# A state space layer on partition halves: two states stacked, channel halves side by side, sums by 64-column matmuls

## What is computed

```
xz = x @ W_in                                  # 256 -> 2 x 512
xc, z = split(xz)
xc = silu(causal_conv4(xc) + conv_b)
proj = xc @ W_xproj                            # 16 + 16 (B) + 16 (C)
dt = softplus(proj_dt @ W_dt + b_dt)           # 512 channels
A = -exp(A_log)                                # 512 x 16
h[t] = h[t-1] * exp(dt[t] * A) + dt[t] * xc[t] * B[t]      # 512 channels x 16 states
y[t] = sum over states (h[t] * C[t]) + D * xc[t]
out = (y * silu(z)) @ W_out
```

## Time and profile before

| | |
|---|---|
| Median of 3 runs | 3203.89 us (3202.26 to 3206.14) |
| Profiled execution, its own time | 3204.56 us |
| Its span | 3203.0 us |
| Busy over the span | PE 2843.9 (89%), PEld 1845.6, VectorE 2080.0 (65%), ACT 1471.0, POOL 1509.9 |
| Granted TensorE clock, mean | 0.957 |
| State space layer's items | from 40.07 to about 1017 us |

### The profile page before, as it was taken

The page is one execution under the profiler, slowest core; times in us unless marked ns, Lnnn a source line. Parts: engine busy times, 40 slices in busy tenths (PEclk is TensorE's granted clock), DMA queues, the critical chain, the costliest instruction groups (busy, mean ns, idle before and its releaser), DMA issues. The chain is left out here.

```text
span 3203.0 us, 41427 instructions
## 1 busy us (share of the span) xinstructions
PE 2843.9 (89%) x14210; PEld 1845.6 (58%) x14210; DVE 2080.0 (65%) x3833; ACT 1471.0 (46%) x2768; POOL 1509.9 (47%) x1192
## 2 busy tenths in 40 slices
PE   6898998998977877899999999978877999999998
PEld 2343343343333664555555555546666888888887
DVE  7899999999998654677777777758863222222221
ACT  5667667666763301366666656545541111111111
POOL 5788788888785553133333333256752111111111
PEclk8999999999999788899999999999888999999999
DMA  7135145145140162212322222110115665556662
GB/s 233 51 108 159 46 116 160 35 125 159 34 136 1 41 211 94 81 42 65 81 63 65 58 50 64 50 59 29 50 63 198 200 203 183 181 181 187 205 199 60
DMA packets 283856, 346.32 MB, mean 108 GB/s; under 512 B 85788, under 2 KB 238552, under 8 KB 283592
## 3 DMA queue, kind: packets, MB, share of 16 engines
q1 hardware_dynamic: 260399, 310.17, 31.3%
q0 software_dynamic: 16704, 27.21, 3.6%
q10 hardware_dynamic: 6544, 6.30, 0.7%
HBM read 234.69 MB, written 107.95 MB: 107 GB/s over the span
## 5 line engine op out<-in xcount | busy, mean ns | idle before, releaser
L542 POOL TENSOR_TENSOR mb_drive<-mb_dtx,mb_b_rep 128x1024 f32<-128x1024 f32 x255 | 597.0, 2355 | 179.9 <-DVE mb_pD L439 87.9
L853 PE MATMUL mb_pY<-mb_hc,ident 128*128 128x512 f32 x1024 | 502.9, 616 | 55.9 <-DVE mb_hc L456 55.5
L1981 DVE TENSOR_REDUCE at_nm_of<-at_pS 128x1 f32<-128x128 f32 (+1 forms) x756 | 401.6, 556 | 135.8 <-PE at_pS L1969 75.8
L3153 POOL DMA_INDIRECT out<-et_y,et_to x71 | 112.0, 1577 | 667.0 <-DVE et_y L3207 411.0
L3197 DVE TENSOR_TENSOR et_mT<-et_silu,et_pU 128x512 f32<-128x512 f32 (+1 forms) x160 | 100.3, 628 | 471.2 <-ACT et_silu L3168 471.1
L3168 ACT ACTIVATE et_silu<-et_pG 128x512 f32<-128x512 f32 (+1 forms) x160 | 87.8, 549 | 658.0 <-PE et_pU L3229 658.0
L853 PEld LDWEIGHTS mb_pY<-mb_hc,ident 128*128 128x128 f32 x1024 | 190.3, 195 | 326.9 <-issue 183.3
L1969 PE MATMUL at_pS<-at_kT,at_qT 128*128 128x128 f32 (+1 forms) x756 | 306.3, 407 | 65.3 <-DVE at_nm_of L1981 53.4
L598 ACT ACTIVATE mb_pD<-mb_dt,mb_a_neg 128x512 f32<-128x512 f32 x384 | 259.6, 688 | 157.3 <-DVE mb_hc L456 146.0
L439 DVE TENSOR_TENSOR_SCAN mb_pD<-mb_pD,mb_drive 128x1024 f32<-128x1024 f32 x128 | 292.7, 2287 | 42.9 <-ACT mb_pD L596 40.2
L445 DVE TENSOR_TENSOR_SCAN mb_pD<-mb_pD,mb_carried,mb_drive 128x512 f32<-128x512 f32 x256 | 314.0, 1271 | 6.8 <-ACT mb_pD L598 6.8
(11 more groups left out here) (491 smaller groups left out, 4984.7 us busy)
## 6 DMA issues: line engine op xcount, KB each, us to landing
t_wg<-in_t_wgT SPq DMA_DIRECT2D x40, 1024.0 KB, 6.3
t_wu<-in_t_wuT SPq DMA_DIRECT2D x40, 1024.0 KB, 8.8
t_wd<-in_t_wdT SPq DMA_DIRECT2D x40, 1024.0 KB, 11.3
mb_b_rep<-mb_rows SPq DMA_DIRECT2D x64, 512.0 KB, 5.6
mb_c_rep<-mb_rows SPq DMA_DIRECT2D x64, 512.0 KB, 4.8
t_h_sorted<-blank SPq DMA_DIRECT2D x6, 4160.0 KB, 20.2
t_h_sorted<-blank SPq DMA_DIRECT2D x18, 1170.0 KB, 6.2
t_h_sorted<-blank SPq DMA_DIRECT2D x12, 1040.0 KB, 5.8
```

Source lines behind the costliest of these rows:

```text
L542: nc.gpsimd.tensor_tensor(drive[G % RINGS][:, :, :], dtx[:, m, :].unsqueeze(1).to_broadcast([P, 2, CH]), b_rep[:, 2 * j:2 * j + 2, :], ALU ...
L853: last = nc.tensor.matmul(pY[:, :], K.ident[:, :], hc[G % RINGS][:, k, :], start=False, stop=(j == PAIRS - 1 and k == 1))
L1981: nc.vector.tensor_reduce(nm_of[t % 2][:, w0 // 512, a, qb:qb + 1], score_bank(t, k)[:, 0:w1 - w0], axis=AX.X, op=ALU.max, negate=True).th ...
```

## The change

An item's two states now lie on the two partition halves (state 2j on partitions 0 to 63, state 2j+1 on 64 to 127), and the tile's two channel halves lie side by side where the two states lay. Then:

- a row of B or C goes to 64 partitions only: `b_rep` and `c_rep` are half as large, and are filled by two transfers of 128 KB each where there was one of 512 KB; the second operand of drive and weighting is repeated over the channel halves;
- dt and dtx are needed as [2 copies on the partition halves, channel half, 512]. They are copied there from SBUF to SBUF, into `dt2` and `dtx2` with TWINS = 3 buffers, by `twins`: four transfers of 128 KB for dt and four for dtx, for each of the 32 tiles. SP issues tile 0's of the next chunk behind the transfers of j = 5, and those of tiles 1 to 3 behind `fill_rows`;
- decay and drive wait for these copies in place of dt and dtx;
- `state_sum` multiplies with `fold` (128 x 64, the sum of the identity's two halves), once for each channel half, into partitions 0 to 63 and 64 to 127 of `pY`; the skip product is split likewise;
- `step_sizes` of the next chunk's tile 0 moves from s = 31 to s = 29;
- A_log is laid out for this on the host.

```diff
+    HP = P // 2
+    TWINS = 3
@@
-        a_neg = sb("a_neg", [P, ME, NST])
+        a_neg = sb("a_neg", [P, ME, 2, PAIRS])
+        fold = sb("fold", [P, HP])
@@
-        b_rep, c_rep = sb("b_rep", [P, NST, CH]), sb("c_rep", [P, NST, CH])
+        dt2, dtx2 = sb("dt2", [P, TWINS, 2, CH]), sb("dtx2", [P, TWINS, 2, CH])
+        b_rep, c_rep = sb("b_rep", [P, PAIRS, CH]), sb("c_rep", [P, PAIRS, CH])
@@ SP
+            def twins(ch, m):
+                nth = ch * ME + m
+                q = nth % TWINS
+                for made, to, s_made, s_to, s_used, per in ((dt, dt2, s_dt, s_dt2, s_dec, 2), (dtx, dtx2, s_dtx, s_dtx2, s_drv, 1)):
+                    eng.wait_ge(s_made, nth + 1)
+                    if nth >= TWINS:
+                        eng.wait_ge(s_used, (nth - TWINS + 1) * PAIRS * per)
+                    for k in range(2):
+                        for h in range(2):
+                            eng.dma_start(to[h * HP:(h + 1) * HP, q, k, :], made[k * HP:(k + 1) * HP, m, :]).then_inc(s_to[q], 16)
@@
-                    eng.dma_start(b_rep[:, 2 * j:2 * j + 2, :], rows_dram[ch % 2][2 * j:2 * j + 2, :].partition_broadcast(P)).then_inc(s_b[j], 16)
+                    for h in range(2):
+                        eng.dma_start(b_rep[h * HP:(h + 1) * HP, j, :], rows_dram[ch % 2][2 * j + h, :].partition_broadcast(HP)).then_inc(s_b[j], 16)
                     if ch > 0:
                         eng.wait_ge(s_hc, last_user + 1)
-                    eng.dma_start(c_rep[:, 2 * j:2 * j + 2, :],
-                                  rows_dram[ch % 2][NST + 2 * j:NST + 2 * j + 2, :].partition_broadcast(P)).then_inc(s_c[j], 16)
+                    for h in range(2):
+                        eng.dma_start(c_rep[h * HP:(h + 1) * HP, j, :], rows_dram[ch % 2][NST + 2 * j + h, :].partition_broadcast(HP)).then_inc(s_c[j], 16)
+                    if j == 5:
+                        twins(ch, 0)
                 fill_rows(K, eng, K.h1_sorted, ch, NCH, s_fill)
+                for m in range(1, ME):
+                    twins(ch, m)
@@ drive (VectorE for item 0, POOL for the others)
+        def twin_made(eng, s_to, nth):
+            eng.wait_ge(s_to[nth % TWINS], 64 * (nth // TWINS + 1))
+
+        def drive_of(unit, ch, m, j, r):
+            return unit.tensor_tensor(drive[r][:, :, :], dtx2[:, (ch * ME + m) % TWINS, :, :],
+                                      b_rep[:, j, :].unsqueeze(1).to_broadcast([P, 2, CH]), ALU.mult)
@@ weigh
-                nc.vector.tensor_tensor(hc[r][:, :, :], pD[r][:, :, :], c_rep[:, 2 * j:2 * j + 2, :], ALU.mult).then_inc(s_hc, 1)
+                nc.vector.tensor_tensor(hc[r][:, :, :], pD[r][:, :, :], c_rep[:, j, :].unsqueeze(1).to_broadcast([P, 2, CH]), ALU.mult).then_inc(s_hc, 1)
@@ VectorE, start
+            nc.vector.tensor_tensor(fold[:, :], K.ident[:, 0:HP], K.ident[:, HP:P], ALU.add).then_inc(s_fold, 1)
@@ POOL, drives
                 if j == 0 or G == 1:
-                    eng.wait_ge(s_dtx, ch * ME + m + 1)
+                    twin_made(eng, s_dtx2, ch * ME + m)
@@ POOL, loop
-                    if s == 31 and ch + 1 < NCH:
+                    if s == 29 and ch + 1 < NCH:
                         step_sizes(eng, nc.gpsimd, ch + 1, 0)
@@ ACT, decay
-                scale = a_neg[:, m, 2 * j + k:2 * j + k + 1]
+                scale = a_neg[:, m, k, j:j + 1]
+                step = dt2[:, (ch * ME + m) % TWINS, k, :]
                 if k == 0:
                     if j == 0:
-                        eng.wait_ge(s_dt, ch * ME + m + 1)
+                        twin_made(eng, s_dt2, ch * ME + m)
@@ ACT, magnitude
                 if ch > 0:
-                    eng.wait_ge(s_drv, (ch - 1) * ITEMS + (m + 1) * PAIRS)
+                    twin_made(eng, s_dt2, (ch - 1) * ME + m)
+                    twin_made(eng, s_dtx2, (ch - 1) * ME + m)
@@ PE, state_sum
-                    nc.tensor.matmul(pY[:, :], skip[:, m, :], xc(ch, m), start=True, stop=False)
+                    for k in range(2):
+                        nc.tensor.matmul(pY[k * HP:(k + 1) * HP, :], skip[:, m, k * HP:(k + 1) * HP], xc(ch, m), start=True, stop=False,
+                                         skip_group_check=True)
                 eng.wait_ge(s_hc, G + 1)
                 for k in range(2):
-                    last = nc.tensor.matmul(pY[:, :], K.ident[:, :], hc[G % RINGS][:, k, :], start=False, stop=(j == PAIRS - 1 and k == 1))
+                    last = nc.tensor.matmul(pY[k * HP:(k + 1) * HP, :], fold[:, :], hc[G % RINGS][:, k, :], start=False, stop=(j == PAIRS - 1),
+                                            skip_group_check=True)
```

More of the change, by code:

```diff
@@ L288, in mamba @@
             sem(n) for n in ("dec", "drv", "scan", "keep", "hc", "y", "fin", "rows", "fill"))
+        s_dt2, s_dtx2 = [sem(f"dt2_{q}") for q in range(TWINS)], [sem(f"dtx2_{q}") for q in range(TWINS)]
+        s_fold = sem("fold")
         s_b = [sem(f"b{j}") for j in range(PAIRS)]
@@ L321, in _ @@
                 loads.append((dst[:, :], io[name].rearrange("(m p) -> p m", p=P)))
-            loads += [(a_neg[:, :, :], io["mb_A_log"].rearrange("(m p) n -> p m n", p=P)),
+            loads += [(a_neg[:, :, :, :].rearrange("p m k j -> p (m k j)"), io["mb_A_log"]),
                       (w_x[:, :, :], io["mb_w_x"].rearrange("(m p) n -> p m n", p=P)),
@@ L349, in _ @@
             for j in range(PAIRS):
-                eng.wait_ge(s_b[j], 16 * NCH)
-                eng.wait_ge(s_c[j], 16 * NCH)
-        ALL_IN = 16 * 7
+                eng.wait_ge(s_b[j], 32 * NCH)
+                eng.wait_ge(s_c[j], 32 * NCH)
+            for q in range(TWINS):
+                uses = len(range(q, NCH * ME, TWINS))
+                eng.wait_ge(s_dt2[q], 64 * uses)
+                eng.wait_ge(s_dtx2[q], 64 * uses)
+        ALL_IN = 16 * 7
+        def twin_made(eng, s_to, nth):
[3 more added lines that the diff above has]
+                                      b_rep[:, j, :].unsqueeze(1).to_broadcast([P, 2, CH]), ALU.mult)
         def normalise(eng, unit, ch):
@@ L426, in first_drive @@
             def first_drive():
[L427 to L430, removed]
+                twin_made(eng, s_dtx2, 0)
+                eng.wait_ge(s_b[0], 32)
+                drive_of(nc.vector, 0, 0, 0, 0).then_inc(s_drv, 1)
             def scans(G):
@@ L445, in scans @@
                     nc.vector.tensor_tensor_scan(pD[r][:, k, :], pD[r][:, k, :], drive[r][:, k, :],
-                                                 carried[:, m, 2 * j + k:2 * j + k + 1], ALU.mult, ALU.add).then_inc(s_scan, 1)
+                                                 carried[:, m, j, k:k + 1], ALU.mult, ALU.add).then_inc(s_scan, 1)
             def weigh(G):
@@ L538, in drives @@
                 if m == 0:
-                    eng.wait_ge(s_b[j], 16 * (ch + 1))
+                    eng.wait_ge(s_b[j], 32 * (ch + 1))
                 if G >= RINGS:
                     eng.wait_ge(s_scan, 2 * (G - RINGS) + 2)
-                nc.gpsimd.tensor_tensor(drive[G % RINGS][:, :, :], dtx[:, m, :].unsqueeze(1).to_broadcast([P, 2, CH]),
-                                        b_rep[:, 2 * j:2 * j + 2, :], ALU.mult).then_inc(s_drv, 1)
+                drive_of(nc.gpsimd, ch, m, j, G % RINGS).then_inc(s_drv, 1)
             inverse_deviation(0)
@@ L577, in keep @@
                 eng.wait_ge(s_hc, G + 1)
-                nc.scalar.copy(carried[:, m, 2 * j:2 * j + 2], pD[G % RINGS][:, :, CH - 1]).then_inc(s_keep, 1)
+                nc.scalar.copy(carried[:, m, j, :], pD[G % RINGS][:, :, CH - 1]).then_inc(s_keep, 1)
             def decay(G, k):
@@ L594, in decay @@
                 if k == 1 and ch % 2 == 0:
-                    nc.scalar.activation(pD[r][:, 1, 1:], dt[:, m, 1:], ACT.Exp, scale=scale)
+                    nc.scalar.activation(pD[r][:, 1, 1:], step[:, 1:], ACT.Exp, scale=scale)
                     nc.scalar.copy(pD[r][:, 1, 0:1], zeros[:, 0:1]).then_inc(s_dec, 1)
                 else:
-                    nc.scalar.activation(pD[r][:, k, :], dt[:, m, :], ACT.Exp, scale=scale).then_inc(s_dec, 1)
+                    nc.scalar.activation(pD[r][:, k, :], step, ACT.Exp, scale=scale).then_inc(s_dec, 1)
             def transposed(ch, k):
@@ L749, in _ @@
             projected(0)
-            nc.scalar.activation(a_neg[:, :, :], a_neg[:, :, :], ACT.Exp).then_inc(s_a, 1)
+            nc.scalar.activation(a_neg[:, :, :, :], a_neg[:, :, :, :], ACT.Exp).then_inc(s_a, 1)
             for m in range(2):
@@ L871, in _ @@
             eng.wait_ge(s_diag, ME * TAPS + ME)
+            eng.wait_ge(s_fold, 1)
             for i in range(NCH):
```

14 lines of the change are left out of this document (9 added, 5 removed).

## The result

The changed kernel takes 3293.38 us (median of 4 runs, 3293.31 to 3295.45) against 3203.07: 1.0282 times as long, 95% interval 1.0264 to 1.0299. The forecast was 3290.

The account below looks back on a forecast made before the run. VectorE bounds the layer's loop, all but 59 us being its own work. Terms 9 + 20.6 + 38.5 + 9 + 21.6 - 10 = 88.7, less about 3, give +86 on 3204.6: 3290 us; range 3228 to 3325.

Parts of the forecast that it names:

- start, to scan 3: Layer's start: row transfers and eight copies issued before drive 0 make scan 3 later, +9 us (bounds +7 and +12).
- step sizes at s=29: On POOL, ahead of drive 29 and waiting for ACT's logarithm: scan 29 late in seven chunks, 20.6 us.
- wait before scan 32, seven: Chunk boundaries: tile 0's copies, issued behind weighting 29, delay drive 32; 5.5 us x 7, 38.5 us.
- wait before scan 35, seven: POOL, s=3: tile 1's step sizes ahead of drive 35 make it late; 1.3 us x 7, 9 us.
- wait before scan 41: Tile 1's copies queue behind the zero fill, then step sizes precede drive 41: 2.9 x 7 and 1.3, 21.6 us.
- faster sums and waits absorbed: 64-column sums on PE save 10 us; about 3 us of waits on ACT disappear in new idle time.
- T: Chunk boundary: moment weighting 29 ends and SP goes on; last dtx issue forecast at T+4.2, drive 32 at T+6.5.
- The fill's term: Tile 1's copies move only after the 4160 KB zero fill lands, 19.4 us after issue; 21.6 us, bounds 0 and 40.
- the 4 us of the longest wait on ACT: VectorE's longest wait on ACT (5.3 us), behind a PE backlog in chunk 0 with four sums: 4 us back.
- B: Rival: copies cost less, overtaking the zero fill and landing in 1.6 us; about 3253 us, chance 0.20.
- C: Rival: the sums' two halves don't run side by side on PE; 3315 us, chance 0.10 (over 3315).
- D: Rival: PE's backlog paces ACT and through it VectorE; 59.3 us come back, down to 3183 us; chance 0.08 (faster).

Follow-up runs that it names:

- e1: The changed kernel with the step sizes of the next chunk's tile 0 back at s=31; 3277.79 us, 1.0240 times the kernel before.
- e7: The changed kernel with tile 0's copies behind j=3 (chunk 0: j=2), the zero fill behind all copies, step sizes still at s=29; 3234.25 us, ratio 1.0036.
- e8: As e7, with the step sizes back at s=31; 3223.36 us, 1.0002 times the kernel before.
- e3: The changed kernel with the zero fill issued behind the copies of tiles 1 to 3; 3276.39 us, 1.0223 times the kernel before.
- e4: The kernel before with sums and skip product as two 64-column matmuls, half of the state sum left out; 3199.48 us, ratio 0.9988.
- e9: The changed kernel again, unaltered, in another group on one chip; 3316.33 us, 1.0316 times the kernel before.
- e11: The changed kernel with the sums as two 128-column matmuls, skip product still split, output not the layer's; 3324.57 us, ratio 1.0341.
- e12: As e8, with chunk 0's copies of tile 0 behind j=0; 3216.36 us, 1.0003 times the kernel before.

## Why the prediction was right, point by point

| term | forecast | measured in the changed kernel |
|---|---|---|
| start, to scan 3 | +9 | +14.7 (66.97 for 52.29) |
| step sizes at s=29 | +20.6 | +20.2 (e1); +7.7 with the copies well placed (e7 less e8) |
| wait before scan 32, seven | +38.5 | +49.9 (6.80 to 7.37 each) |
| wait before scan 35, seven | +9 | +8.7 |
| wait before scan 41 | +21.6 | +16.4; e3 gives 18.6 |
| faster sums and waits absorbed | -13 | -12.3, what is left of the layer's +97.6 |

The rows are not independent of each other: e1's 20.2 us contain 5.8 that go before scan 32 (the experiment above), and the last row is a remainder. By VectorE's waits, it holds about 6 us of waits on PE and some 8 of small waits on ACT that the new idle time covers.

The mechanism held in the terms of the loss; in the gain of the sums I left out that ACT takes back part of it (e4). An in-order SP puts the copies behind weighting 29 and behind the fill, an in-order POOL hands on its lateness when the next step sizes come (scans 35 and 41), and VectorE, without slack, pays it, all but what small waits absorb. VectorE's idle time in the loop was forecast near 140 us and is 159.5 less the start's 15.6.

Two terms were mis-sized, for one reason. I took "0.36 and then 0.47" for an issue, from transfers to 128 partitions. A copy of 64 partitions, and a row broadcast to 64, holds SP 0.64 us from one issue to the next (four in 2.46 and the gap to the next; a pair in 1.24). At a boundary the last dtx copy's issue begins at T+5.6 (T is 180.21), not T+4.2, and drive 32 at T+8.1, not T+6.5: 1.6 us x 7. In the start 24 issues take 15 us and not 11, and the eight copies twice 2.51 us and not 3.8: 5.7 us. The landing itself was the 2.3 us that I had taken (median of the dtx copies from 160 to 190 us; 2.6 for dt).

The fill's term came out 5 us smaller: the fill landed after 18.1 us, where I had taken 19.4 from the kernel before, and nothing waited in chunk 0. With a fill of 19.2 us (e9) the same waits come to 22.5 us, chunk 0's 0.75 among them, against my 21.6.

The layer is +97.6, where I had +86: the errors of the terms, +5.7, +11.4 and -5.2 the largest, partly cancel. That the medians differ by 90.3 only, and so come within 4 us of the forecast, is luck: what follows the layer took 6.7 us less than before in the two profiled executions. On the chip of e9 the changed kernel's median was 101.2 us above that of before.

The sums: L853's 502.9 us were to halve and went to 349.4, 1.36 us an item, not 1.06. The halves do run side by side: four records in 1.08 us at 2.4 GHz. But the granted clock fell, and then they take 1.97 (below). From the Trainium skill's rule on weight loads and strict order (TensorE: Matmul & The Clock Gate, Part 3, The mechanism) I had worked out an estimate of 1.5 us at full clock; the trace does not bear it out for these two column strips, whose four records end 1.08 us after the first one's start. On the old kernel the gain was half of what I took (-4.8 of the layer for -10, bounds 0 and -59): the 6 us of waits on PE came (11.0 to 4.8), the 4 us of the longest wait on ACT did not (5.3 to 5.0), and of what other waits gave, ACT took 6.8 us back at the boundary. In the changed kernel the form is worth more, 11.7 us (e11 against e9).

Rivals: B's way (copies overtaking the fill) is refuted by e3; C's (the halves one after the other) by the 1.08 us; D's by e4. That the change is slow by its order and not by its copies is shown by e8 and e12: with the same copies and broadcasts, the whole time can't be told from that of the kernel before on the same chip.

## What to carry to other kernels

What a transfer cost here was what stood ahead of it in its issuer's program. Before moving data by DMA between two engines, write down for the first use of each buffer the moment the data exist, what the issuing queue waits for in front of the copy, the number of issues ahead and the time of each, and any large transfer in the same queue; here 84.8 of the layer's 97.6 us of loss went when tile 0's copies were issued earlier and the fill last (e7), and next to none was left with the step sizes back at s=31 (e8, e12). A step moved earlier (s=29) gains nothing if its consumer is gated elsewhere, and costs if its own input is not there yet. And the relief of an engine that isn't the bound is worth little: 163 us less progress of the sums (230 expected) gave 4.8.

## What the runs showed of the hardware that was not expected

**The granted clock fell with PE's load.** From 46 to 1010 us the mean granted clock is 0.97 in the kernel before and 0.85 in e4_before64, whose items come at the same pace and differ in the sums alone. In the changed kernel, on windows of 2 us around the boundary (PE busy, the next columns PEld, VectorE, ACT and POOL, then the clock as a share of 2.4 GHz):

```profile
182.00:184.00 2.00, 0.97 (x6) 0.20 (x4) 1.52 (x2) 0.00 (x0) 0.00 (x0) 1.00 0.75 226
184.00:186.00 2.00, 0.66 (x4) 0.00 (x0) 0.00 (x0) 0.22 (x1) 0.00 (x0) 1.00 0.87 209
186.00:188.00 2.00, 0.82 (x1) 0.50 (x2) 0.00 (x0) 1.91 (x7) 0.00 (x0) 0.67 0.81 189
188.00:190.00 2.00, 1.25 (x2) 0.00 (x0) 0.00 (x0) 1.20 (x2) 1.71 (x1) 0.50 0.65 186
```

PE had been little busy in the stall (1.6 of the 4 us from 182 to 186), and the clock fell from 1.00 to 0.50 (1.2 GHz) there. The same four records of one item stand at either level in PE's time line:

```profile
181.47 1.08 PE L889 MATMUL mb_pY<-mb_hc,mb_fold 128*64 128x512 f32 x4
...
194.30 1.97 PE L889 MATMUL mb_pY<-mb_hc,mb_fold 128*64 128x512 f32 x4 [5.05 <-DVE mb_hc L488]
```

At 1.97 us an item the split sums cost what the full ones cost before (502.9 us for 256 items, nearly all at the higher level). So part of what the 64-column form saves is given back by the clock: from 46 us to near the layer's end it is 0.92 with the full sums (e11_after128) and 0.81 with the split ones (e9_after). What the split sums would gain with the clock held at the higher level no run shows.

**The time of an SP issue differed with the transfer and with what was in flight:** 0.64 us for 128 KB on 64 partitions, whether a broadcast from DRAM or a copy from SBUF to SBUF, and 0.47 for a broadcast of 512 KB to 128 (which of size and partitions decides was not tested). Behind the fill of 4160 KB four issues took 8.68 us, of which the first held SP for most:

```profile
199.18 6.35 SPq L346 DMA_DIRECT2D mb_dt<-mb_dt  x1
```

**The fill's speed differed with the chip and with the kernel.** Kernels with the copies had it in 18.1 to 18.3 us on the first chip of the experiments, 19.9 to 20.6 on the second and 18.9 to 19.2 on the third. But e4_before64, with the SP program of the kernel before, took 19.9 on the first. What of the kernel makes it slower there isn't shown.
